# One graph transformer layer on one core: an earlier neighbour-list front, and the output rows finished inside the last 48 chunks of the attention loop

## The reference, cut to what matters

```
xn = layernorm(x)
x  = x + gnn(xn, edges) + mix(xn)       # two branches
x  = x + ffn(layernorm(x))              # mixture of 8 experts
gnn: q,k,v = xn@W.T + b (8 heads of 32); for each edge s->d: sim = q[d].k[s]/sqrt(32)
     softmax over the edges of d, weighted sum of v[s]; then @Wo.T + bo
mix: linear attention: k,v normalised per head (8 of 64); dots = k^T v over all nodes;
     out = q @ dots / N, then @w_out.T + b_out
ffn: logits = h@gate_w + gate_b; idx = argmax; pos = running count of idx in node order
     (at most C = 977 rows per expert are kept); y = (relu(h@w1[e]+b1)@w2[e]+b2)*prob
     nan_to_num(y); dropped rows give 0
```

## Time and profile before

| | us |
| --- | --- |
| median of 3 runs | 2956.17 (2955.47 to 2956.94) |
| the profiled execution | 2953.88 |
| its span, first to last instruction | 2952.6 |
| front, up to the first key/value gather | 265.0 |
| from there to the last gather's issue | 2115 |
| last gather to first expert matmul | 191 |
| experts | 381 |

### The profile page before, as it was taken

How to read it: one execution, slowest core, us unless ns; L and a number is a source line. 1 busy time by engine, 2 the same in 40 slices (tenths; PEclk the granted TensorE clock), 3 DMA queues, 4 the chain that set the end, 5 groups by cost and what they waited for, 6 DMA issues and landing times. The chain is left out here.

```text
span 2952.6 us, 37856 instructions
## 1 busy us (share of the span) xinstructions
PE 2191.0 (74%) x9653; PEld 1727.9 (59%) x9654; DVE 2449.9 (83%) x3309; ACT 1078.0 (37%) x4488; POOL 1974.0 (67%) x1979
## 2 busy tenths in 40 slices
PE   5753777787766777887877767777885655599998
PEld 4551555455555665665666545555664435499988
DVE  5763878888888899999999888899999987566765
ACT  2300211112366666666666411111111114256463
POOL 4175777777777777777777777777777727335453
PEclk9975887888899899989999878999898875599999
DMA  8517888888877777777777788888887735423341
GB/s 249 182 43 156 238 238 239 241 244 247 230 217 218 218 218 218 220 217 218 218 220 217 226 233 248 249 253 253 252 246 223 210 121 171 117 69 82 82 92 15
DMA packets 262373, 579.18 MB, mean 196 GB/s; under 512 B 57174, under 2 KB 141582, under 8 KB 262136
## 3 DMA queue, kind: packets, MB, share of 16 engines
q0 software_dynamic: 151392, 469.80, 57.6%
q1 hardware_dynamic: 101606, 99.38, 10.7%
q10 hardware_dynamic: 9296, 9.05, 0.9%
HBM read 512.54 MB, written 69.78 MB: 197 GB/s over the span
## 5 line engine op out<-in xcount | busy, mean ns | idle before, releaser
L1128 POOL DMA_INDIRECT wide<-kv_d,arena x1099 | 1053.8, 959 | 334.8 <-issue 326.9
L1463 PE MATMUL ps<-wide,arena 128*128 128x264 f32 x2432 | 699.0, 450 | 176.5 <-DVE wide L1566 176.4
L1463 PEld LDWEIGHTS ps<-wide,arena 128*128 128x128 f32 x2432 | 534.4, 225 | 329.4 <-DVE wide L1566 216.7
L1128 POOL DMA_INDIRECT arena<-kv_d,arena x539 | 516.3, 958 | 164.2 <-issue 160.6
L1255 ACT ACTIVATE ps<-wide 128x256 f32 x229 | 88.8, 388 | 1259.0 <-DVE arena L1532 1255.0
L1535 DVE TENSOR_REDUCE arena<-arena 128x64 f32<-128x2048 f32 x229 | 523.4, 2286 | 7.9
L1532 DVE TENSOR_TENSOR arena<-wide,ps 128x2048 f32<-128x2048 f32 x153 | 349.4, 2284 | 114.1 <-DMA wide<-kv_d,arena 113.8
L1463 PE MATMUL ps<-arena 128*128 128x264 f32 x1216 | 338.1, 439 | 88.7 <-DVE arena L1566 88.5
L140 PE MATMUL ps<-halves 128*128 128x256 f32 (+2 forms) x2304 | 360.7, 318 | 2.0 <-DVE halves L1801 2.0
L1566 DVE TENSOR_TENSOR wide<-wide,ps 128x2112 f32<-128x2112 f32 x152 | 356.7, 2347 | 0.0
L1463 PEld LDWEIGHTS ps<-arena 128*128 128x128 f32 x1216 | 259.5, 218 | 160.8 <-DVE arena L1566 108.9
(11 more groups left out here) (348 smaller groups left out, 3255.2 us busy)
## 6 DMA issues: line engine op xcount, KB each, us to landing
wide<-kv_d,arena POOLq DMA_INDIRECT x1099, 3.8
arena<-in_w SPq DMA_DIRECT2D x16, 1024.0 KB, 5.7
kv_d<-wide SPq DMA_DIRECT2D x49, 260.0 KB, 2.4
arena<-xt_d SPq DMA_DIRECT2D x82, 128.0 KB, 3.5
arena<-kv_d,arena POOLq DMA_INDIRECT x539, 3.8
h_d<-wide SPq DMA_DIRECT2D x7, 903.0 KB, 5.1
row_d<-wide SPq DMA_DIRECT2D x7, 896.0 KB, 9.1
xs_d<-wide SPq DMA_DIRECT2D x49, 128.0 KB, 3.6
```

The lines of the kernel that those rows point to most:

```text
L1128: e.indirect_dma_start(out=kvb[k][:, j, :], out_offset=None, in_=kv_d, in_offset=bass.IndirectOffsetOnAxis(ap=ixb[k][:, j:j + 1], axis=0)) ...
L1463: m = e.matmul(psE[(k + 1) % 3][:, 0:264], ident, kvb[b][:, j, 256:ROW], start=(j == 0), stop=(j == J - 1))
```

## The change

Two parts, in one edit.

**The front.** `firsts` is read straight from the input dst by the first three DMAs of SP's queue and no longer from the padded copy. The first group's normalisation moves behind the histogram. `ranks` starts ahead of the tile loop, each quarter of the gathered pieces has a semaphore of its own, and the generator waits for quarter q only PACE[q] = 3, 6, 5, 5 pumps after the one before. Two pumps per tile come from tile 19 on (WAIT_ROWS = 18). The source ids are stored in four pieces (OWN), each at a set pump (OWN_STEPS), during the projection pass, and the gather of sorted rows waits for the last group's rows to be stored and no longer for the whole pass.

**The output rows.** The aux rounds move from behind `join` to the end of the loop (48 chunks), and do more: PE adds the attention output to the base in PSUM (`rows_of`), ACT writes the finished row, its mean, variance and normalised row (`rows_out`), PE transposes that and multiplies by the gate (`turned_of`), ACT stores the logits (`turned_out`), and SP stores h_d rows of 265 values (the row, 8 logits, index). `step(s)` handles tile s - 3 and the logits of tile s - 5. GpSimd writes rows to out at the end of its program in the block. DVE works out the expert codes at the end of its own (`experts_by_row`). The pass of seven groups, base_d and its reloads go. The softmax weight of the chosen expert is now worked out in the expert stage from the gathered logits.

```diff
-WAIT_ROWS = 40
+WAIT_ROWS = 18
+PACE = (3, 6, 5, 5)
+OWN = ((0, 16), (16, 32), (32, 41), (41, 49))
+OWN_STEPS = (17, 31, 39, 46)
+        dma(Y, fi_i[:, 0:12], dst[0:12 * 128 * 128].rearrange("(a p j) -> p a j", p=128, j=128)[:, :, 0], s_fi, ...)
...
-        t_fi = dma(Y, fi_i, dst_d.rearrange("(a p) j -> p a j", p=128)[:, :, 0], s_fi, allow_slow_non_contiguous=True)
...
         def ranks():
-            take_rows(v(V.tensor_copy(blki, blk)))
-            for _ in range(WAIT_ROWS):
-                yield
-            wait(V, (s_row, s_row.n))
-            for c0, c1 in QUARTERS:
+            take_rows(t_blk)
+            for q, (c0, c1) in enumerate(QUARTERS):
+                for _ in range(PACE[q]):
+                    yield
+                wait(V, (s_row[q], s_row[q].n))
...
-            while not projected:
+            while 6 not in t_rn:
                 yield
-            t_ids = store_own(t_own)
-            wait(V, t_ids)
+            while None in t_ids:
+                store_own()
...
+        more[0] = ranks()
+        pump()
         for grp in range(7):
...
-            between[0]()
-            with turns(aux):
-                for k in range(RING):
-                    body(k, aux=True)
-            between[1]()
             with turns(val(e, cnt_)):
                 for k in range(RING):
                     body(k)
+            between()
+            with turns(AUX - 1):
+                for k in range(RING):
+                    body(k, aux=RING + k)
...
             late_tiles(e, ns, tl, late_tile)
+            for c in range(NT - 3):
+                e.wait_ge(e_bc, c + 2)
+                t_o[0] = s_o.inc(e.indirect_dma_start(out=out, out_offset=..., in_=qi[:, c, 0:256], in_offset=None), 16)
...
+            def rows_out(i, tile):
+                e.wait_ge(e_bp, bd)
+                e.wait_ge(e_hs[i], hs)
+                link(e.activation(qsf[:, bass.ds(val(e, tile, 48) * QI, 256)], x2_ps, ACT.Identity, accum_out=fs[0]))
+                link(e.activation(fs[1], fs[0], ACT.Copy, scale=-1.0 / 256))
+                link(e.activation(junk, x2_ps, ACT.Square, bias=fs[1], accum_out=fs[2]))
+                link(e.activation(fs[3], fs[2], ACT.Ln, bias=epsc, scale=1.0 / 256))
+                link(e.activation(fs[4], fs[3], ACT.Exp, scale=-0.5))
+                link(e.activation(fs[5], fs[1], ACT.Copy, scale=fs[4]))
+                e.activation(hrow[i][:, 0:256], x2_ps, ACT.Identity, bias=fs[5], scale=fs[4]).then_inc(e_bc, 1)
+                e.activation(hrow[i][:, HW - 1:HW].bitcast(i32), permS[:, bass.ds(val(e, tile, 48), 1)], ACT.Copy)
...
+            def rows_of(i, tile, written, count):
+                e.matmul(x2_ps, ident, xr[i], start=True, stop=False)
+                for c in range(2):
+                    e.matmul(x2_ps, xm3[i][:, c, :], M[:, c, :], start=False, stop=False)
+                e.matmul(x2_ps, ones[0:2, :], brow, start=False, stop=False)
+                e.matmul(x2_ps, ident, qsf[:, bass.ds(val(e, tile, 48) * QI, 256)], start=False, stop=True).then_inc(e_bp, 1)
...
+            def turned_of(gate, turn, i):
+                if gate:
+                    for c in range(2):
+                        e.matmul(lg_ps, hT[:, c, :], gw[:, c, :], start=(c == 0), stop=False)
+                    m = e.matmul(lg_ps, ones[0:1, :], gbias[0:1, :], start=False, stop=True)
+                if turn:
+                    e.transpose(tq_ps[:, 0:128], hrow[i][:, 0:128], ident)
+                    m = e.transpose(tq_ps[:, 128:256], hrow[i][:, 128:256], ident)
```

More of the change, by code:

```diff
@@ L361, in gps_layer_kernel @@
         t_hist = sp.inc(m)
+        wait(V, t_x[0])
+        spread(xbuf[0], range(7))
+        t_r0 = root(0)
         t = v(V.memset(cnt[:, 0:1], 0.0))
@@ L388, in gps_layer_kernel @@
         rest = R1[:, 10596:10646]
-        s_row = sem("s_row")
+        s_row = [sem(f"s_row{i}") for i in range(4)]
         QUARTERS = [(0, 13), (13, 26), (26, 39), (39, 50)]
-        more = [None]
+        more, steps, t_own, t_ids = [None], [], [None] * 4, [None] * 4
         def pump(n=1):
@@ L956, in aligned, with rounds @@
             return nc.Fori(0, end, engines=(kind,))
-        def rounds(e, pre, body, step, between, aux=AUX, kind=None, before=None):
+        def rounds(e, pre, body, step, between, kind=None, before=None):
             def turns(end, hint=False):
@@ new lines, in turned_out @@
+            def turned_out(logits, turn, i, tile):
+                e.reg_add(tq, tq, 1)
+                e.wait_ge(e_tq, tq)
+                if logits:
+                    e.activation(hrow[i][:, 256:264], lg_ps, ACT.Copy)
+                    e.activation(qsf[:, bass.ds(val(e, tile, 48) * QI + 256, 8)], lg_ps, ACT.Copy).then_inc(e_lg, 1)
+                    e.reg_add(ln, ln, 1)
+                if turn:
+                    e.activation(hT, r3(tq_ps, 128), ACT.Copy).then_inc(e_hc, 1)
+                else:
+                    e.wait_ge(e_lg, ln)
+                    e.nop().then_inc(e_hc, 1)
@@ L1324, in stored @@
                 e.activation(dsb, finite, ACT.Copy, scale=0.0).then_inc(e_dz, 1)
-            rounds(e, "a_", body, join, (first_out, last_out), AUX - 1, mybir.EngineType.Activation, stored)
-            for _ in range(2):
+            rounds(e, "a_", body, join, first_out, mybir.EngineType.Activation, stored)
+            for k in range(2):
                 record()
                 tile_end()
+                step(AUX * RING + k)
+            for s_ in range(NT + 1, NT + 5):
+                step(s_)
             def late_row():
@@ L1721, in turn_h @@
-        def turn_h(u):
-            pt = ps[4 + u % 3]
-            wait(T, t_h[u], t_hT.get(u - 3), t_fin)
-            for k in range(2):
-                m = T.transpose(pt[:, k * 128:(k + 1) * 128], hr[u // 7 % 2][:, u % 7, k * 128:(k + 1) * 128], ident)
-            t_ = sp.inc(m)
-            wait(S, t_, t_lg.get(u - 3))
-            t_hT[u] = a(S.activation(hT[u % 3], r3(pt[:, 0:256], 128), ACT.Copy))
-        def gate(u):
-            wait(T, t_hT[u], t_ld.get(u // 7 - 2))
-            for k in range(2):
-                m = T.matmul(gate_ps[u // 7 % 2][:, u % 7 * 8:u % 7 * 8 + 8], hT[u % 3][:, k, :], gw[:, k, :], start=(k == 0), stop=(k == 1))
-            t_lg[u] = sp.inc(m)
```

599 lines of the change are left out of this document (291 added, 308 removed).

## The result

| | before | changed |
|---|---|---|
| median of 3 runs, us | 2956.17 (2955.47 to 2956.94) | 3041.05 (3034.88 to 3041.06) |
| profiled execution, span, us | 2952.6 | 3033.7 |
| mean granted TensorE clock | 0.875 | 0.867 |

The change makes the kernel slower: ratio 1.028, 95% interval 1.0257 to 1.0303. Forecast were 2822, with 2795 to 2862 as the range.

The account below looks back on a forecast made before the run. GpSimd's unbroken gathers bound the loop, with DVE setting the pace near its end and a late sort delaying its start. 2953.9 - 57 (front) + 5 (loop) - 82.5 (behind) = 2819.4, median 2822; range 2795 to 2862.

Parts of the forecast that it names:

- The map of the kernel: Whole kernel: GpSimd gathers without stopping for 2115 us, late DVE stalls show one for one, experts stay at 381 us.
- The sign of the front: Ahead of the loop: first key/value gather at 208, a gain of 57 us; bounds 185 and 241.
- the part behind the loop: Loop end to experts: first expert matmul at +68 against +150.7, gain 82.5 us, bounds 70 and 92.
- the one for the loop's tail: Last 48 chunks: finishing output rows inside the loop costs 5 us in all, bounds 0 and 35.
- Rival (b): Last 48 chunks: ACT waits for PE, DVE for ACT; 1.5 us a chunk, 72 us, total 2889; chance 0.07.
- the mix rounds: Argument from earlier loop rounds: ACT had 5.9 us of work in each 8.40 without holding up DVE.
- rival (c): Last 48 chunks: clock stays at 1.2 GHz, PE needs about 15 us a chunk, 288 more, 3105; chance 0.01.
- gains of 139 us: Front and behind the loop: expected gains, lost from 2.9 us more a chunk over 48 chunks.
- it did not fall with more work: TensorE's granted clock: 0.88 with 29.9 us of PE work in 50, 0.93 with 40.6.
- ACT has six steps left after the last chunk: Behind the loop: four steps have the 3.1 us chain; last row sent at +23.5, barrier open at about +28.5.
- I take 114 us: Front from 88.5: DVE's tiles, sort and tables end at 202; 100 us packed without a gap, 146 end to end.
- Rival (a): Front: PE and DVE wait for one another, loop starts at 235 or later, gain 30 or less, 2850; chance 0.09.

Follow-up runs that it names:

- number 7: Changed kernel with SP's row store first, ACT's store wait late, and PE's PSUM bank freed after ACT's first step: 2854.3 us, 0.967 of before.
- Experiment 2: Changed kernel with the front's hunks taken back, so the tail alone: 3058.5 us, 1.035 of the kernel before.
- 3: Changed kernel with SP storing the finished row tile before waiting for PE and reading the next inputs: 2899.7 us, 0.983 of before.
- 6: Changed kernel with only PE's PSUM bank freed after ACT's first step, later steps reading the SBUF copy: 2896.7 us, 0.981 of before.
- The five experiments: Front edits, one run each: more sort steps 2906.1, stores on ACT 2890.3 (both on 5); one product less 2850.8, later compares 2851.3 (on number 7), plus sort step between 2849.2.
- 5: Changed kernel with SP's row store first and ACT's wait for the old store late: 2896.2 us, 0.982 of the kernel before.

## Why the prediction was wrong

**What was right.** The map of the kernel: GpSimd without a pause for 2115 us before, DVE's stalls in the last 48 chunks showing nearly one for one (135.7 us of waits, 150.7 us of loop), the row pointers at 88, the source gathers until 161, the experts unchanged. The sign of the front, and of the part behind the loop. With the ring cut, number 7, the loop was 2149.0 against my 2159 and the part behind it 78.0 against 70.

**The step that failed most** is the one for the loop's tail: "ACT gets a chain ... I take 5 us over all 48 chunks, bounds 0 and 35". It summed ACT's steps (4.0 us) and PE's (7.5 us) and asked whether each fits into 8.4 us alone. Both do, and number 7 shows it. It did not follow what one waits for in the other, nor SP at all: what SP issues in a chunk, and in which order, stands in no term. The store of a row tile stood behind a wait for PE, and ACT's next tile behind that store: 1.3 + 4.5 us that no engine's busy time contains. What was put at 5 us measured 150.7, four times the upper bound. Experiment 2 shows that it is the tail, 3 and 6 show the place: take the store or the bank out of the ring, and 132 or 119 of them are gone.

**The rival was named, with the wrong size.** Rival (b) had ACT's chain wait for PE in the same chunk, and DVE for ACT, at 1.5 us a chunk. It was 3.1 (150.7 / 48), and the argument against it, the mix rounds, did not hold: there ACT had more work, but in the chunk of the earlier trace rows its waits are for DVE (1.05 and 2.49 us), and none is for a store or for PE. How full an engine can be says nothing on how long a ring through it takes.

Slower than before needed less than rival (c) said. It worked out 2.9 us a chunk as the price at which all gains are lost, from gains of 139 us. The gains came out at 70 us (19.8 and 50.6), so 1.5 us a chunk was enough.

**The clock.** Against rival (c) I wrote of the clock that "it did not fall with more work". From 2100 to 2340 us, in the changed kernel and then before:

```profile
2100.00:2340.00 240.00, 185.25 (x659) 138.00 (x658) 159.48 (x182) 73.15 (x317) 115.68 (x121) 0.79 0.59 167
```

```profile
2100.00:2340.00 240.00, 170.01 (x615) 126.68 (x613) 233.58 (x267) 29.99 (x141) 182.12 (x191) 0.89 0.80 233
```

It was 0.79 against 0.89, with more waiting and somewhat more work (PE busy 185 of 240 us against 170). A single stretch of 50 us says little here: from 2200 to 2250 the kernel before had 0.80 itself. The clock never stayed at 1.2 GHz, as (c) had it, but 16 of 25 groups of five matmuls ran there in whole or in part and took 4.2 to 5.2 us instead of 2.8. With the ring cut (number 7) it was 0.99.

**Behind the loop.** "ACT has six steps left after the last chunk, of which four have the 3.1 us chain": the last row was to be out at +23.5 and the barrier to open at +28.5. It opened at +55.9, since the six steps left came every 7.5 to 11.4 us (ACT's L1317 at 2551.1, 2562.4, 2571.4, 2581.0, 2588.5 and 2596.1) and not every 4 to 5. With the ring cut it opened at +32.1 (DVE's last step ended at 2394.6):

```profile
2426.66 0.57 DVE L1887 TENSOR_TENSOR arena<-ps,arena 128x392 f32<-128x392 f32 x1 [4.81 <-PEq L1835]
```

So 24 of the 27 us are the same mistake. The other 5 us of this term are from barrier to experts; their cause is open.

**The front.** The step that failed is "I take 114 us, nearer the packed end since the sort's waits fall beside tiles: 202". The work was sized rightly, at 100 us for DVE, and its overlap was not. From 90 to 230 us in the changed kernel it was busy (third number)

```profile
90.00:230.00 140.00, 95.82 (x539) 74.92 (x539) 100.13 (x332) 26.29 (x64) 70.04 (x62) 0.82 0.53 135
```

100.1 us. But these took 143, from 90 to 232.8, and not 114. That is the bound for everything laid end to end (234), so the tiles and the sort covered next to nothing of one another's waits. With SP's stores ahead of the indices, a further 6 us that stand in no term, the first gather came at 245.2, later than even the bound of 241. Rival (a) said that the front would pack badly, with 0.09. Why it does is argued and not shown: in one queue in fixed order a sort's step that waits holds up the tile behind it, and a tile's round trip over ACT and PE the sort. The five experiments moved the start by -6.7 to +7.8 us, none by what one bound would give.

**The range** was worked out from bounds of single terms, and the bound of 35 us for the tail came from the same model as the 5, while that of 241 for the front left out the stores in SP's queue. A wait whose releaser is in no row of before is not bounded by the rows of its neighbours.

## What to carry to other kernels

When work moves into a loop, write down for each step not only its engine's time but what releases it, through every queue, SP's too, and add up each closed ring; compare that with the period, beside the busy times. Stores belong first in a queue, reads for a later round behind them, and a buffer is to be given back behind its first reader that can copy it. If no engine is full in a stretch, look for the ring in the waits; here the wait that a DMA ended (ACT's at L1317) led to it.

## What the runs showed of the hardware that was not expected

- A store of 132.5 KB from SBUF took 4.4 us from issue until ACT went on, with the DMA engines 0.60 busy; the median over 49 of them was 3.8 us to landing. It takes 0.36 us of SP's issuing, and its landing shows only where somebody's next step needs the buffer. The Trainium skill (DMA: Bandwidth & Descriptors, "Anatomy of one DMA — SWDGE (gpsimd) path") has, for GpSimd's path, about 2.0 us fixed and the rest by size at 436 GB/s; an estimate by that fit is 2.3 us for this size. It is not a statement on SP's queue, and the trace does not agree for a store there beside gathers: 3.8.
- A third of a projection's matmuls left out shortened PE's busy time by 6.7 us of 96, and the granted clock of that stretch went down from 0.82 to 0.71 (one execution each).
- The same matmuls with the waits between them taken away (numbers 5 and 7, 2100 to 2340) ran at a granted clock of 0.99 instead of 0.87: 985 records in 216.4 us against 923 in 220.1.
